# A graph-attention layer and a gated graph layer on one core: row gathers first, value gathers second

## The reference

```python
h = relu(layernorm(x))
wh = (h @ weight).reshape(n, H, F)              # H = 4 heads, F = 32
e = leaky_relu(parent[:, None] + child[None], 0.2)
att = softmax(where(adj > 0, e, -9e15), axis=1) # over the neighbours
x = x + einsum(att, wh)                         # layer 1
h = relu(layernorm(x))
msg = relu((adj @ h) @ W_msg.T + b_msg)         # layer 2
x = x + gru_cell(msg, h, W_ih, W_hh, b_ih, b_hh)
```

## Time and profile before

| | |
|---|---|
| median of 3 runs | 1160.31 us (1157.52 to 1160.41) |
| the profiled execution, by the clock of the runs | 1159.31 us |
| its span, first to last instruction | 1157.6 us |
| main loop with filling and drain | some 97 to 872 us |
| layer 2 | from some 872 us on |
| HBM traffic in the loop | 388 to 428 GB/s |
| mean granted TensorE clock | 0.821 |

### The profile page before, as it was taken

The page is one execution under the profiler, slowest core; times in us unless marked ns, Lnnn a source line. Parts: engine busy times, 40 slices in busy tenths (PEclk is TensorE's granted clock), DMA queues, the critical chain, the costliest instruction groups (busy, mean ns, idle before and its releaser), DMA issues. The chain is left out here.

```text
span 1157.6 us, 14697 instructions
## 1 busy us (share of the span) xinstructions
PE 679.1 (59%) x4141; PEld 523.0 (45%) x4141; DVE 586.4 (51%) x2487; ACT 686.2 (59%) x723; POOL 592.6 (51%) x598
## 2 busy tenths in 40 slices
PE   0076555765665566566566566655332776777774
PEld 0064334554454454354354444444331565555563
DVE  4632524656656646747647647557331244433443
ACT  0497866886887887788778778772210333233331
POOL 0021074464564654654744744735705777777770
PEclk9997887888788788778878878876555989899998
DMA  7748999999999999999999999951101222222220
GB/s 237 308 149 306 428 401 413 412 411 416 393 396 413 390 413 407 389 406 405 393 413 403 392 413 398 388 224 20 42 5 44 60 67 68 57 68 70 67 66 25
DMA packets 58623, 311.92 MB, mean 269 GB/s; under 512 B 15577, under 2 KB 32994, under 8 KB 42210
## 3 DMA queue, kind: packets, MB, share of 16 engines
q1 hardware_dynamic: 30434, 277.37, 58.8%
q0 software_dynamic: 19712, 30.02, 10.7%
q10 hardware_dynamic: 8448, 4.20, 1.2%
HBM read 298.82 MB, written 12.71 MB: 269 GB/s over the span
## 5 line engine op out<-in xcount | busy, mean ns | idle before, releaser
L457 ACT ACTIVATE ind<-adj_in 128x4144 bf16<-128x4144 int32 (+1 forms) x128 | 461.9, 3609 | 39.1 <-DMA adj_in<-in_adj 22.8
L397 POOL DMA_INDIRECT rows_in<-wh_table,idx x192 | 198.2, 1032 | 304.4 <-DVE val_idx L869 250.7
L602 PE MATMUL ps<-ind,bit_w 128*128 128x296 bf16 (+1 forms) x1792 | 312.2, 340 | 0.0
L602 PEld LDWEIGHTS ps<-ind,bit_w 128*128 128x128 bf16 x1792 | 206.9, 115 | 89.9
L1030 POOL DMA_INDIRECT rows_in<-g_table,idx x192 | 197.6, 1029 | 91.3 <-issue 54.0
L401 POOL DMA_INDIRECT vals_in<-in_adj,val_idx x192 | 183.6, 956 | 58.6 <-issue 58.6
L799 DVE MAX8 cand<-ps 128x8 f32<-128x148 f32 x256 | 61.9, 304 | 117.6 <-PE ps L602 117.2
L598 PE MATMUL ps<-idx_r,idx_w 128*128 128x296 bf16 x128 | 44.2, 346 | 129.8 <-ACT ind L457 129.6
L1164 DVE TENSOR_SCALAR ownT<-iota,edge_row 128x128 f32<-128x128 f32 x64 | 14.7, 324 | 152.6 <-DMA rows_in<-g_table,idx 152.5
L598 PEld LDWEIGHTS ps<-idx_r,idx_w 128*128 128x128 bf16 x128 | 15.8, 123 | 140.4 <-ACT ind L457 126.5
L619 PE MATMUL ps<-rest,tri 128*128 128x4 f32 x32 | 9.0, 352 | 115.0 <-DVE rest L833 115.0
(11 more groups left out here) (220 smaller groups left out, 1514.7 us busy)
## 6 DMA issues: line engine op xcount, KB each, us to landing
adj_in<-in_adj SPq DMA_DIRECT2D x64, 2072.0 KB, 15.0
adj_in<-in_adj SPq DMA_DIRECT2D x64, 2024.0 KB, 14.0
wh_table<-t_buf POOLq DMA_DIRECT2D x16, 264.0 KB, 3.0
g_table<-t_buf ACTq DMA_DIRECT2D x16, 256.0 KB, 25.1
out<-adj_in SPq DMA_DIRECT2D x16, 256.0 KB, 2.3
rows_in<-wh_table,idx POOLq DMA_INDIRECT x192, 6.7
vals_in<-in_adj,val_idx POOLq DMA_INDIRECT x192, 6.7
rows_in<-g_table,idx POOLq DMA_INDIRECT x192, 2.8
```

What stands on the lines that cost most here:

```text
L397: nc.gpsimd.indirect_dma_start(out=rows_in[:, par, t, k, :], out_offset=None, in_=wh_table, in_offset=bass.IndirectOffsetOnAxis(ap=idx[:, ...
L457: nc.scalar.activation(ind[:, t % 2, a:b], adj_in[:, slot, 0:b - a].bitcast(I32), ACT.Relu, bias=1.0, scale=-1.0, accum_out=empty[:, bass. ...
L602: ins = nc.tensor.matmul(o[:, 0:w], bit_w[:, b, :], ind[:, t % 2, c0:c0 + w], start=False, stop=(b == BITS - 1))
```

## The change

`gather` issues its twelve row gathers first, still on `gathered`, and then its twelve value gathers on a new pair of semaphores, `values_in`. `child_logits` waits for the rows alone and copies `valid3` as the mask. The product with the values moves to a new function, `keep_values(s - 3, 1 - par)`, called behind `add_first(s - 3)`: it waits for `values_in`, makes the product, compares it with 0, takes the difference from `valid3` and reduces it into a fifth row of `checks`, so that a listed entry with a value not over 0 sends the kernel to the general path. `val_idx` gets two buffers.

```diff
--- before.py
+++ after.py
@@ -119,11 +119,12 @@
         idx = sb("idx", [P, G, 3], I32)
         row_f = sb("row_f", [P, G, 3])
         row_i = sb("row_i", [P, G, 3], I32)
-        val_idx = sb("val_idx", [P, G, 3], I32)
+        val_idx = sb("val_idx", [P, 2, G, 3], I32)
         tile_row = sb("tile_row", [P, G])
         tile_low = sb("tile_low", [P, G])
-        checks = sb("checks", [P, 4, NG])
-        over = sb("over", [P, 10])
+        checks = sb("checks", [P, 5, NG])
+        over = sb("over", [P, 12])
+        unsure = sb("unsure", [P, G, 3])
         over1 = sb("over1", [P, 1])
         empty = sb("empty", [P, 2 * T])
         over_f = sb("over_f", [1, 1])
@@ -263,6 +264,7 @@
         recv_done = sem("recv_done")
         idx_done = sem("idx_done")
         gathered = [sem(f"gathered{i}") for i in range(2)]
+        values_in = [sem(f"values_in{i}") for i in range(2)]
         crest_done = sem("crest_done")
         c_mm = sem("c_mm")
         pm_done = sem("pm_done")
@@ -398,10 +400,12 @@
                                 out=rows_in[:, par, t, k, :], out_offset=None, in_=wh_table,
                                 in_offset=bass.IndirectOffsetOnAxis(ap=idx[:, t, k:k + 1], axis=0),
                             ).then_inc(gathered[par], 16)
+                    for t in range(G):
+                        for k in range(3):
                             nc.gpsimd.indirect_dma_start(
                                 out=vals_in[:, par, t, k:k + 1], out_offset=None, in_=adj_values,
-                                in_offset=bass.IndirectOffsetOnAxis(ap=val_idx[:, t, k:k + 1], axis=0),
-                            ).then_inc(gathered[par], 16)
+                                in_offset=bass.IndirectOffsetOnAxis(ap=val_idx[:, par, t, k:k + 1], axis=0),
+                            ).then_inc(values_in[par], 16)
 
                 def store(q, par):
                     pool.wait_ge(table_rows, q + 1)
@@ -866,15 +870,14 @@
                     V.tensor_scalar(tile_low[:], tile_low[:], float(G * P), None, ALU.add)
                     link(V.tensor_copy(row_i[:], row_f[:]))
                     link(V.tensor_scalar(row_i[:], row_i[:], int(np.log2(N)), None, ALU.logical_shift_left))
-                    V.tensor_tensor(val_idx[:], row_i[:], idx[:], ALU.bitwise_or).then_inc(idx_done, 1)
+                    V.tensor_tensor(val_idx[:, par], row_i[:], idx[:], ALU.bitwise_or).then_inc(idx_done, 1)
                     for t in range(G):
                         ins = V.tensor_scalar(ownT[:, par, t, :], iota1[:], recv[:, t, K - 1:K], None, ALU.is_equal)
                     link(ins)
 
                 def child_logits(s, par):
-                    dve.wait_ge(gathered[par], (s - par) * (3 * G * 2 * 8) + 3 * G * 2 * 16)
-                    link(V.tensor_tensor(nbr_val[:, tiles(s * G), :], vals_in[:, par], valid3[:, par], ALU.mult))
-                    link(V.tensor_scalar(mask[:], nbr_val[:, tiles(s * G), :], 0.0, None, ALU.is_gt))
+                    dve.wait_ge(gathered[par], (s - par) * (3 * G * 8) + 3 * G * 16)
+                    link(V.tensor_copy(mask[:], valid3[:, par]))
                     V.tensor_tensor(cm[:, :, :, 0:H], rows_in[:, par, :, :, D:TW],
                                     mask[:].unsqueeze(3).to_broadcast([P, G, 3, H]), ALU.mult)
                     link(V.tensor_copy(cm[:, :, :, H], mask[:]))
@@ -936,6 +939,14 @@
                         ins = V.bn_aggr(mv[:, t, :], stats[:, t, :])
                     ins.then_inc(var2_done, 1)
 
+                def keep_values(s, par):
+                    dve.wait_ge(values_in[par], (s - par) * (3 * G * 8) + 3 * G * 16)
+                    val = nbr_val[:, tiles(s * G), :]
+                    link(V.tensor_tensor(val, vals_in[:, par], valid3[:, par], ALU.mult))
+                    link(V.tensor_scalar(unsure[:], val, 0.0, None, ALU.is_gt))
+                    link(V.tensor_tensor(unsure[:], valid3[:, par], unsure[:], ALU.subtract))
+                    V.tensor_reduce(checks[:, 4, bass.ds(s, 1)], unsure[:].rearrange("p g k -> p (g k)"), AX.X, ALU.max)
+
                 def finish_norm(s):
                     dve.wait_ge(sd2_done, s + 1)
                     link(V.reciprocal(rs1[:, tiles(s * G)], sd[:]))
@@ -950,6 +961,7 @@
                         decode(s - 1)
                     if "g" in do:
                         add_first(s - 3)
+                        keep_values(s - 3, 1 - par)
                     if "c" in do:
                         search(s, 0)
                     if "t" in do:
@@ -975,12 +987,12 @@
 
                 schedule(dve, body)
 
-                V.tensor_reduce(over[:, 4:5], empty[:], AX.X, ALU.max)
-                link(V.tensor_reduce(over[:, 0:4], checks[:], AX.X, ALU.max))
-                for n, bound in enumerate((0.5, float(1 << IBITS), float(NEI0), P + 0.5, PIECE + 0.5)):
-                    ins = V.tensor_scalar(over[:, 5 + n:6 + n], over[:, n:n + 1], bound, None, ALU.is_ge)
+                V.tensor_reduce(over[:, 5:6], empty[:], AX.X, ALU.max)
+                link(V.tensor_reduce(over[:, 0:5], checks[:], AX.X, ALU.max))
+                for n, bound in enumerate((0.5, float(1 << IBITS), float(NEI0), P + 0.5, 0.5, PIECE + 0.5)):
+                    ins = V.tensor_scalar(over[:, 6 + n:7 + n], over[:, n:n + 1], bound, None, ALU.is_ge)
                 link(ins)
-                V.tensor_reduce(over1[:], over[:, 5:10], AX.X, ALU.max).then_inc(over_done, 1)
+                V.tensor_reduce(over1[:], over[:, 6:12], AX.X, ALU.max).then_inc(over_done, 1)
                 dve.wait_ge(over_mm, 1)
                 link(V.tensor_reduce(over_f[:], ps[0:1, 0, 0:P], AX.X, ALU.max))
                 link(V.tensor_copy(over_i[:], over_f[:]))
```

## The result

The changed kernel takes 1177.51 us (median, 1166.46 to 1183.72) against 1160.18 us for the kernel before on the same chip. The ratio is 1.014, 95% interval 1.0096 to 1.0183: slower by 17 us. The four executions lie 17 us apart, and the faster ones had the higher mean granted clock (0.825 at 1166.46 us, 0.808 at 1183.72); even the fastest is above all four of the kernel before (at most 1160.41). The profiled execution took 1174.07 us, with a span of 1172.4 us.

What follows compares the result with a forecast made beforehand. It took the ring of PE packs and VectorE's search up to `rest`, 44.37 us a group, as the bound. 1159.3 + 40.3 + 0.8 - 1.9 - 13.7 = 1184.8 us, given as 1185, range 1155 to 1192.

Steps and rivals of the forecast that it cites:

- the ring: Main-loop chain of PE packs and VectorE's search of tile 3 up to `rest`, each step releasing the next; 44.4 us.
- The bound: Main loop: waits set the time, not loads; PE waits 7.3 us a group for VectorE's `rest`.
- `keep_values`, 0.81 us: VectorE, between `add_first` and `search(s, 0)`: added operations cost 0.81 us a group, bounds 0.65 to 1.0, nothing hiding them.
- Its wait, the loop's other parts: In the loop: wait for values, shorter `child_logits` and earlier rows each give 0; load order -0.3 to +0.3 us a group.
- The clock, +3.1 us a group: PE's packs in the loop start later against the clock's steps and run longer: groups 3.1 us above 44.37.
- long pack: PE pack of tile 1 or 2 lengthened by the clock, some 6.5 us against 5.14; one and a half to two foretold a group.
- (c): Rival, main loop: only one long pack in most groups, 1.5 us a group, 1164 us; chance 0.12.
- the forecast case: Main loop 2.6 to 3.6 us a group longer, giving 1178 to 1192 us; chance 0.62.
- The drain, -13.7 us: Last group after the loop: `child_logits` needs only rows, VectorE goes on at 830.5, not 844.2; bounds -12.3 to -14.0.
- (a): Rival, main loop: late packs win back half of each delay from the clock; groups 44.37 to 44.5, 1147.6 us; chance 0.12.
- (b): Rival, main loop: clock steps move along with the work, so costs just add up; 1156.9 us; chance 0.13.
- (d): Rival, drain: the twelve rows cannot be waited for alone, so 13.7 us is added to any case; chance 0.01.

Runs made afterwards that it cites:

- e4: Kernel before plus one linked operation on 12 elements between `add_first` and `search(s, 0)`: 1459.36 us, ratio 1.0058.
- e6: Kernel before without the two reductions of `decode` into `checks`, 0.5 us less in each group: 1432.75 us, ratio 0.9915.
- e2: Changed kernel with rows and values gathered alternately again, on their two semaphores: 1455.23 us, ratio 1.005 to the kernel before.
- e1: Order-only kernel: kernel before with row gathers first, values second, one semaphore, no `keep_values`: 1447.21 us, ratio 0.9987.
- e10: Changed kernel measured again, on one chip with the moved kernel: 1181.45 us, ratio 1.0203 to the kernel before at 1158.08 us.
- e9: Moved kernel: changed kernel with `keep_values` at the end of the body before, the last group's behind `add_first`: 1160.46 us, ratio 1.0025 to the kernel before.
- e11: Changed kernel with eight list-mask instructions of VectorE written as two, `keep_values` still behind `add_first`: 1448.62 us, ratio 0.9969 to the kernel before.
- e12: Moved compact kernel: `keep_values` at the body's end and eight list-mask instructions written as two: 1443.49 us, ratio 0.9944 to the kernel before.

## Why the prediction was right

It gave 1185 us, 1155 to 1192, slower with a chance of 0.71. The median is 1177.5 and on another chip 1181.5. The direction came from the mechanism that was forecast, work in the ring that costs more than itself; that the number is within 8 us is in part luck, as three errors cancelled.

**The bound.** Right. The ring stands in the changed kernel with the same steps, and each change of VectorE's stretch on one chip moved the time the same way: +0.6 to 0.7 us a group +11.8 us (`e4`), -0.5 us -10.8 us (`e6`), +0.95 us +8.0 us (`e2` against `e1`) and +21.0 us (`e10` against `e9`).

**`keep_values`, 0.81 us.** Mis-sized: 0.95 us (0.92 to 0.96 in all bodies but the first, 0.77), inside its bounds of 0.65 to 1.0. Its spacings (0.17, 0.21, 0.32) are those that the sum took from the earlier trace rows, 0.70 in all from L945 to L948. Short was the step that gave the reduction 0.08 to 0.10: behind it `search(s, 0)` starts after 0.25 us. VectorE's stretch grew by less, from 14.33 to 14.86 us, since two operations of `decode` that took 0.42 and 0.43 us in the group of the earlier trace rows now took 0.23 and 0.22. No step of the prediction had that; the order-only and the moved compact kernel show the same 13.89 us without `keep_values`, and most groups of the moved one do (others 14.1 to 14.3). Why these operations differ is open.

**Its wait, the loop's other parts.** Right at zero: no wait for `values_in`, none for rows; the new order of the gathers cost nothing (`e1`).

**The clock, +3.1 us a group.** That packs turn long by the clock was right, the size was off. Packs of tile 1 were foretold at 6.5 us against 5.14, and they came at 6.4; the same happened to packs of tile 2, once in the first run and four times in `e10`. But "one and a half to two long packs in each group" was wrong: of the eleven groups in the table, seven had one long pack in the first run (each of the first three, then every second) and nine in `e10`, and none had two. That is the picture of rival (c), one long pack in most groups; the first run's +2.0 us a group lies below the 2.6 with which the forecast case begins, and only `e10` with +2.7 is in it. The ring did not come to rest at one length but alternates: 45.0 without a long pack, 47.1 with one. The steps of a group, start to start, in us:

| step | before | long group | short group |
|---|---|---|---|
| `rest` to the pack of tile 1 | 0.70 | 0.70 | 0.70 |
| to the pack of tile 2 | 10.48 | 11.8 | 10.48 |
| to the pack of tile 3 | 13.39 | 13.68 | 13.27 |
| to the search of tile 3 | 5.48 | 6.03 | 5.6 |
| to the next `rest` | 14.33 | 14.86 | 14.86 |

So +2.0 us a group on the mean in the first run, +2.7 in the second, where the prediction had 3.1 within bounds of 1.9 to 3.8. In the loop that is +22.9 us against +39.2 foretold (13 x 3.1 + 0.8 - 1.9); in `e10` it is +32.3. Following the ring with one price for each late pack gave too many of them: in no group of the four traces in the table above are the packs of tile 1 and of tile 2 both long, and behind a long pack of tile 1 the next ones cost 0.4 and 0.6 us more, not 1.5.

Why groups take turns is not settled, and a rival stands. In the first run and in `e10` tile 1's pack is long in each of the ten groups that follow a stall of VectorE at L913 and in none of the eight between them (in `e10` tile 2's is long in three of these). But both runs have long packs ahead of the first stall, and in `e9` only two of the five stalls are followed by one. So part of the surplus of 2.0 to 2.7 us may come with the larger loop and not with the place of `keep_values`; `e11`, which has no such loading, ran on a chip where the clock's share cannot be read.

**The drain, -13.7 us.** The gain at the wait was foretold within 1 us: `child_logits` starts 18.4 us after the first gather of its group is issued (foretold 19, before 32.9), with no wait for a gather, so 14.5 us come there. What was wrong is what is late next. The sum asked only VectorE. The timeline of PE in the drain of the changed kernel:

```profile
856.31 1.12 PE L651 MATMUL ps<-ident,h 128*128 128x128 f32 x4 [7.47 <-ACT h L479]
858.10 2.08 PE L657 MATMUL ps<-wT,hT 128*128 128x128 f32 x8 [0.68 <-ACT hT L486]
859.97 1.82 PE L615 MATMUL ps<-cm_rest,ownT 128*128 128x70 f32 x8
```

`rest_logits` (L615) is queued on PE behind `message_rows` of the group before (L657), and that waits for ACT's `h2_rows` and `h2_columns`, which follow from the same `finish_norm` that VectorE has just done. Before, the wait for values covered all of it, and VectorE's own wait at this place was 2.07 us; now it is 6.36. Of the 14.5 us, 4.3 are given back there at once. One operation less in `child_logits` saves 0.2, the work behind that wait is 0.9 us shorter (23.0 against 23.9, 0.8 of it in the matmuls of `maxima`, 1.06 against 1.88 us), and so the drain is 11.3 us shorter, not 13.7.

**The rest.** Layer 2 +1.2 us and the start +1.9 us were not in the sum; the step that held them at zero was silent. No run takes them apart.

**Errors that cancelled.** Against its own profiled execution: the loop was 16 us too dear, the drain's gain 2.4 too large, and 3 us were missing, which leaves 1174.1 where 1184.8 was foretold.

**The rivals.** (a), absorbed: out, the group is 2.0 to 2.7 us longer. The short groups come near it (45.0 with 0.95 us more work). (b), plain sum: out. With 0.95 us and the measured drain it gives 1159.3 + 13.3 - 11.3 = 1161.3. On the chips where the kernel before takes some 1450 us the sum is near the profiled loops of `e11` and `e12`, and too small for `e4` (9 us against 11.8) and `e6` (7 against 10.8). A pack at full clock took 3.91 us; the 44 packs of eleven groups took 218.0 us before, 46 us more than 44 x 3.91, and another 15.3 and 19.1 us more after the change, 3.1 and 3.9% of that stretch of 489 us. The Trainium skill, "TensorE: Matmul & The Clock Gate", Part 1, has the ramp penalty under 1% of a typical kernel span; these traces do not agree, since 46 us are already 4% of the whole span of 1157.6 us. (c), half: nearest in its picture, too small in its price: it took 1.5 us a group and named 1164, the measured mean is 2.0. (d): out, the rows can be waited for alone.

## What to carry to other kernels

Find the ring before placing work: 0.95 us of small VectorE operations behind `add_first` cost 21 us on a chip like the first and 5 to 13.5 us on another, against the same ones at the end of the body, where the engine waits anyway. When the wait that ends last is taken away, list for each engine in the chain what stands in front of the next step in its own queue, not only on the engine that waited: here PE's queue took back 4.3 of 14.5 us. Where single matmul stretches run at two clock levels, the groups of a ring can grow by two to three times the work put in (2.0 and 2.7 us for 0.95 here), and from one odd group in the trace that could be bounded but not foretold.

## What the runs showed of the hardware

- The same kernel takes 1158 to 1160 us on two chips and 1444 to 1455 us on three others, with nothing else changed: the traffic is 295 GB/s and not 402 in the window of 300 to 700 us, with the DMA engines less busy (0.81, 1.01), and PE has single waits of 1.7 to 2.5 us for nothing that the profile shows. There a change showed its sign and not its size: groups had one mean length, 61.45 to 61.47 us over ten groups, with 0.95 us (`e2`, `e11`) and with 0.6 to 0.7 us (`e4`) more in VectorE's stretch.
- With up to 314 instructions of VectorE in the loop's two bodies the whole run loads 17 instruction packets, with 316 and more 42: 25 more, or five for each of the five returns to the loop's start. With 42, VectorE stands still for 1.6 to 2.5 us longer at the start of every second body of the changed kernel on the chips of 1160 us (5.9 to 6.7 against 4.3 us), and up to 6.9 us in the moved one. In the changed kernel that moved the search of tile 3 by some 0.6 us in all; in the moved kernel by 4.1 us. Whether it is what keeps the moved kernel from its gain, or the waits for loads, stays open.
- A single operation on 12 elements, put behind `add_first`, moved the next one by 0.39 us (`e4`), where such operations start 0.21 us apart elsewhere.
- The spell at half clock around tile 1's pack was 6.8 us long in the group of the kernel before that was read, and 10.2 and 6.8 us in two groups that follow each other in the changed kernel, with nearly the same idle time of PE in it (8.26 and 8.37 us).
